# Scans that read PSUM, B products on GpSimd, and a new order of all steps, in an eight-layer network

## The reference

```python
A = -jnp.exp(A_log)
dA = jnp.exp(jnp.einsum('bld,dn->lbdn', delta, A))
dBu = jnp.einsum('bld,bln,bld->lbdn', delta, Bm, u)
def step(h, t):
    dA_t, dBu_t, c_t = t
    h = dA_t * h + dBu_t
    return (h, jnp.einsum('bdn,bn->bd', h, c_t))
_, ys = jax.lax.scan(step, h0, (dA, dBu, Cs))
y = jnp.moveaxis(ys, 0, 1) + u * Dp
```

## Time and profile before

| | |
|---|---|
| median of 3 runs | 1476.47 us (1473.23 to 1480.88) |
| the profiled execution | 1478.42 us, its span 1476.5 us |
| mean granted TensorE clock | 0.931 of full |
| busy share | PE 89%, DVE 72%, ACT 62%, POOL 42% |
| DMA | 82.88 MB moved |

### The profile page before, as it was taken

How to read it: one execution, slowest core, us unless ns; L and a number is a source line. 1 busy time by engine, 2 the same in 40 slices (tenths; PEclk the granted TensorE clock), 3 DMA queues, 4 the chain that set the end, 5 groups by cost and what they waited for, 6 DMA issues and landing times.

```text
span 1476.5 us, 25953 instructions
## 1 busy us (share of the span) xinstructions
PE 1307.9 (89%) x8638; PEld 924.5 (63%) x8638; DVE 1061.3 (72%) x3854; ACT 911.8 (62%) x2506; POOL 624.0 (42%) x637
## 2 busy tenths in 40 slices
PE   8324767987679999999999999999999999999998
PEld 4112445654446766776777776777778788875665
DVE  4998998588987478778347877559949769774334
ACT  5625687778664686756456778645758756664221
POOL 0002255532552365544545554744643433421744
PEclk9756789988879899999999999999999999999999
DMA  6777320105402001100100000020110000006230
GB/s 244 186 177 171 78 52 1 51 1 164 115 15 82 32 2 51 60 2 1 58 1 1 1 2 20 40 117 1 59 76 2 2 1 2 1 1 210 48 93 22
DMA packets 21788, 82.88 MB, mean 56 GB/s; under 512 B 1852, under 2 KB 8252, under 8 KB 19352
## 3 DMA queue, kind: packets, MB, share of 16 engines
q1 hardware_dynamic: 21656, 81.23, 18.8%
HBM read 77.88 MB, written 3.33 MB: 55 GB/s over the span
## 4 chain that ended last, share of the span: by engine, by line
PE 57%; DVE 26%; ACT 8%; issue 4%; POOL 3%; DMA 1%; SPq 0%; DVEq 0%; POOLq 0%; ACTq 0%
PE bank L888 49%; DVE arena L1559 7%; PE bank L892 7%; ACT arena L1321 5%; DVE arena L1726 5%; DVE arena L1797 2%; ACT L1321 2%; DVE arena L2056 2%; DVE arena L1795 2%; DVE arena L2049 1%; DVE arena L1565 1%; DVE stats L1573 1%; DMA arena<-cf 1%; DVE arena L1818 1%; DVE arena L1562 1%
## 5 line engine op out<-in xcount | busy, mean ns | idle before, releaser
L1321 ACT ACTIVATE arena<-arena 128x128 f32<-128x128 f32 (+2 forms) x792 | 347.7, 442 | 78.5 <-DVE arena L1797 54.9
L1321 ACT ACTIVATE arena<-bank 128x512 f32<-128x512 f32 (+4 forms) x378 | 202.7, 571 | 226.5 <-PE bank L888 139.4
L888 PE MATMUL bank<-XT,W 128*128 128x512 f32 (+1 forms) x752 | 292.6, 524 | 0.0
L2139 POOL TENSOR_TENSOR arena<-arena 128x256 f32<-128x256 f32 x192 | 121.0, 630 | 359.0 <-DVE arena L1812 357.9
L888 PEld LDWEIGHTS bank<-W,arena 128*128 128x128 f32 (+1 forms) x1888 | 233.5, 196 | 62.6 <-issue 40.1
L888 PE MATMUL bank<-arena 128*32 128x256 f32 (+8 forms) x2912 | 246.6, 347 | 21.4 <-ACT arena L1321 8.3
L888 PE MATMUL bank<-W,arena 128*128 128x128 f32 (+2 forms) x1888 | 246.1, 281 | 18.4 <-POOL arena L2112 6.0
L888 PEld LDWEIGHTS bank<-arena 128*32 128x32 f32 (+4 forms) x2912 | 162.3, 157 | 106.1 <-issue 73.0
L892 PE MATMUL bank<-CF,arena 128*128 128x128 f32 x1312 | 193.9, 289 | 37.0 <-POOL arena L2140 24.8
L2112 POOL TENSOR_TENSOR arena<-arena 128x512 f32<-128x512 f32 (+1 forms) x108 | 172.8, 1622 | 115.0 <-DVE arena L1559 56.1
L892 PEld LDWEIGHTS bank<-CF,arena 128*128 128x128 f32 x1312 | 158.3, 148 | 87.8 <-issue 58.2
(11 more groups left out here) (123 smaller groups left out, 1581.0 us busy)
## 6 DMA issues: line engine op xcount, KB each, us to landing
arena<-rep SPq DMA_DIRECT2D x62, 512.0 KB, 7.9
arena<-rws SPq DMA_DIRECT2D x8, 2048.0 KB, 7.3
arena<-rws SPq DMA_DIRECT2D x4, 1792.0 KB, 7.6
W<-w SPq DMA_DIRECT2D x2, 2124.0 KB, 8.3
arena<-rws SPq DMA_DIRECT2D x8, 384.0 KB, 10.7
W<-w SPq DMA_DIRECT2D x1, 2692.0 KB, 9.1
W<-w SPq DMA_DIRECT2D x1, 2256.5 KB, 9.3
rep<-arena SPq DMA_DIRECT2D x4, 512.0 KB, 4.8
```

Source lines behind the costliest of these rows:

```text
L888: return e.matmul(o, lhsT, rhs, start=start, stop=stop, skip_group_check=True)
L1321: return e.activation(o, a, func, **kw)
L2139: e.tensor_tensor(px[:, :, 0:128], px[:, :, 0:128], rec[:, :, 0:1].to_broadcast([128, 2, 128]), ALU.mult)
```

## The change

In "0.da" ScalarE writes the decays into a PSUM bank (role A, opened by the ScalarE step and held until "0.st" has scanned it) and not into the slot; a new need lets it run at most two states ahead of the scans. The scans read the bank. "0.bc" copies only B to SBUF; the bank with C stays open until the last "0.ac" of the chunk, and the product with C reads it there. The product with B is a GpSimd step of its own ("0.db") for the 62 states that come by DMA; the two that come by matmul keep it on VectorE. The scheduler counts banks for all engines now.

```diff
-                        own(tt(h, h, s0(c, 8), ALU.mult))
-                        on.wait_ge(*after("dA", "0.da", c, n))
-                        on.wait_ge(*own.last())
-                        for q in range(2):
-                            qs = slice(q * 256, (q + 1) * 256)
-                            own(e.tensor_tensor_scan(h[:, qs], dA[:, qs], h[:, qs], 0.0, ALU.mult, ALU.add))
-                    on.wait_ge(*emptied(u("c", "0.bc", c)))
-                    on.wait_ge(*own.last())
-                    tt(h, h, s0(c, 16), ALU.mult).then_inc(has["hc"], 1)
+                    else:
+                        on.wait_ge(*after("dB", "0.db", c, n))
+                    on.wait_ge(*after("dA", "0.da", c, n))
+                    ins = e.tensor_tensor_scan(h[:, 0:256], bank[a.i][:, 0:256], h[:, 0:256], 0.0, ALU.mult, ALU.add)
+                    if by_pe(c, n):
...
+                    else:
+                        own(ins)
+                    e.tensor_tensor_scan(h[:, 256:512], bank[a.i][:, 256:512], h[:, 256:512], 0.0, ALU.mult, ALU.add
+                                         ).then_inc(done[a.i], 1)
+                    on.wait_ge(*filled(cc))
...
+                    tt(h, h, bank[cc.i][:, :], ALU.mult).then_inc(has["hc"], 1)
```

```diff
-                        act(dA, dA, ACT.Exp, scale=am[:, g:g + 1], bias=am[:, 16 + g:17 + g]).then_inc(has["dA"], 1)
+                        steps_ = ring0(c, n)[:, 0:512]
+                    on.wait_ge(*free(a))
+                    act(bank[a.i][:, :], steps_, ACT.Exp, scale=am[:, g:g + 1], bias=am[:, 16 + g:17 + g]).then_inc(has["dA"], 1)
```

```diff
+                elif name == "0.db":
+                    h = ring0(c, n)[:, 512:1024]
+                    on.wait_ge(*repeated(c, n))
+                    on.wait_ge(*emptied(u("b", "0.bc", c)))
+                    e.tensor_tensor(h, h, s0(c, 8), ALU.mult).then_inc(has["dB"], 1)
```

The needs and the banks:

```diff
+HELD = {("0.bc", 0): [("c", 0, ("0.ac", 3, 0), 1, 1)], ("0.ac", 0): [("Y", 0, ("0.y", 0, 0), 4, 1)], ("1.pv", 0): [("Y", 0, ("1.y", 0, 0), 8, 1)],
...
+for _q in range(16):
+    HELD["0.da", _q] = [("A", 0, ("0.st", _q, 0), 0, 1)]
...
+            add("0.da", q, (by, q), ("0.a", 0, PREP), *([("0.st", q - 2)] if q >= 2 else []))
+            if by == "0.rp":
+                add("0.db", q, (by, q), ("0.bc", 0))
...
-                k = len(opened(x)) if g == "P" else 0
+                k = len(opened(x))
```

```diff
-         [(0, 2), (1, 2), (0, 3), (1, 3), (2, 2), (2, 3), (3, 2), (3, 3), (4, 2), (4, 3), (5, 2), (5, 3),
+         [(0, 2), (0, 3), (1, 2), (1, 3), (2, 2), (2, 3), (3, 2), (3, 3), (4, 2), (4, 3), (5, 2), (5, 3),
```

```diff
             load_x(2)
             e.dma_start(CF[:, 0:FIRST], cf[:, 0:FIRST]).then_inc(d_c, 16)
+            e.dma_start(W[0][:, 0:FIRST0], ws[0][:, 0:FIRST0]).then_inc(d_w[0], 16)
             load_x(0)
-            e.dma_start(W[0][:, 0:FIRST0], ws[0][:, 0:FIRST0]).then_inc(d_w[0], 16)
             load_x(1)
             e.dma_start(W[0][:, FIRST0:ws[0].shape[1]], ws[0][:, FIRST0:]).then_inc(d_late, 16)
+            e.dma_start(CF[:, FIRST:], cf[:, FIRST:]).then_inc(d_c2, 16)
             load_w(1)
-            e.dma_start(CF[:, FIRST:], cf[:, FIRST:]).then_inc(d_c2, 16)
```

More of the change, by code:

```diff
@@ L42 @@
 W_IN = {0: 0, 4: 0, 6: 0, 1: 1, 2: 1, 3: 1, 5: 1, 7: 1}
-CONSTS = [("ident", 128), ("one", 128), ("rows8", 128), ("mhalf", 20), ("cosk", 256), ("sink", 256), ("cosq", 256), ("sinq", 256), ("low", 128),
+CONSTS = [("ident", 128), ("mhalf", 20), ("one", 128), ("rows8", 128), ("cosk", 256), ("sink", 256), ("cosq", 256), ("sinq", 256), ("low", 128),
           ("stm", 384), ("relum", 384), ("outm", 384), ("offd", 384), ("early", 64), ("hm", 4)]
-FIRST = 404
+FIRST = 148
 FIRST0 = 1816
@@ L130 @@
 THIRDS = {1: 5, 4: 5, 6: 4}
-HELD = {("0.ac", 0): [("Y", 0, ("0.y", 0, 0), 4, 1)], ("1.pv", 0): [("Y", 0, ("1.y", 0, 0), 8, 1)],
+HELD = {("0.bc", 0): [("c", 0, ("0.ac", 3, 0), 1, 1)], ("0.ac", 0): [("Y", 0, ("0.y", 0, 0), 4, 1)], ("1.pv", 0): [("Y", 0, ("1.y", 0, 0), 8, 1)],
         ("4.pv", 0): [("Y", 0, ("4.y", 0, 0), 8, 1)], ("6.o", 0): [("out", 0, ("6.e", 0, 0), 8, 1)]}
 BLOCKS, SHARED, HIDDEN = {1: 8, 5: 8, 7: 14}, {1: 1, 5: 0, 7: 2}, {1: 4, 5: 4, 7: 5}
+for _q in range(16):
+    HELD["0.da", _q] = [("A", 0, ("0.st", _q, 0), 0, 1)]
 for _q in range(BEGIN[1]):
@@ L236, in stage_steps @@
                 add(by, q, ("0.wr", 0), *([("0.ac", (q - STATES) // 4)] if q >= STATES else []))
-            add("0.da", q, (by, q), ("0.a", 0, PREP))
-            add("0.st", q, ("0.da", q), (by, q), ("0.bc", 0), *([("0.st", q - 1)] if q else []))
+            add("0.da", q, (by, q), ("0.a", 0, PREP), *([("0.st", q - 2)] if q >= 2 else []))
+            if by == "0.rp":
+                add("0.db", q, (by, q), ("0.bc", 0))
+            add("0.st", q, ("0.da", q), ("0.db" if by == "0.rp" else by, q), ("0.bc", 0), *([("0.st", q - 1)] if q else []))
         for k in range(4):
@@ L333 @@
 TASKS = [[(s, 0) for s in range(8)], [(s, 1) for s in range(8)],
-         [(0, 2), (1, 2), (0, 3), (1, 3), (2, 2), (2, 3), (3, 2), (3, 3), (4, 2), (4, 3), (5, 2), (5, 3),
+         [(0, 2), (0, 3), (1, 2), (1, 3), (2, 2), (2, 3), (3, 2), (3, 3), (4, 2), (4, 3), (5, 2), (5, 3),
           (6, 2), (6, 3), (7, 2), (7, 3)]]
 AHEAD = {
[4 rows of a table removed]
-    (0, PREP): 67.31, (1, PREP): -869.94, (2, PREP): -782.64, (3, PREP): -77.67, (4, PREP): 246.56, (5, PREP): -616.95, (6, PREP): 195.78, (7, PREP): 842.21}
-URGENT = {
[9 rows of a table removed]
-LANDS = {("0.n", 2): 5.0, ("0.n", 0): 5.5, ("0.n", 1): 8.5, ("0.w", PREP): 8.0, ("0.a", PREP): 8.0, ("0.f", PREP): 8.0, ("0.b", PREP): 10.0}
[4 rows of a table added]
+    (0, PREP): -73.44, (1, PREP): 22.35, (2, PREP): -97.02, (3, PREP): 94.50, (5, PREP): -111.58, (6, PREP): 334.41, (7, PREP): 182.60}
+URGENT = {
[6 rows of a table added]
+    -36.44, "load": -56.09}
+LANDS = {("0.n", 2): 3.9, ("0.n", 0): 10.0, ("0.n", 1): 11.3, ("0.w", PREP): 8.6, ("0.a", PREP): 8.6, ("0.f", PREP): 8.6, ("0.b", PREP): 25.0}
 OVER = {4: (0,), 5: (1,), 6: (4,), 7: (3, 5)}
@@ L623, in group0, with by_pe @@
             return q % 4 * 4 + q // 4
+        def by_pe(c, q):
+            return c == BEGIN[0] and q < BEGIN[1]
         def repeated(c, q):
@@ L913, in _ @@
                     on.wait_ge(d_w[s], 16)
+                if name in ("0.ac", "0.b"):
+                    on.wait_ge(d_c2, 16)
                 if name in ("0.y", "0.h", "0.o", "0.b"):
@@ L969, in _ @@
                                  ring0(c, 4 * n + j)[:, 512:1024], n == 0, n == 3)
+                        if n == 3 and j == 0:
+                            ins.then_inc(done[uses["c", "0.bc", c, 0].i], 1)
                     ins.then_inc(full[b.i], 1)
@@ L1384, in _ @@
                 elif name == "0.bc":
-                    for b, k in ((u("b", name, c), 8), (u("c", name, c), 16)):
-                        evict(b, s0(c, k), bank[b.i][:, :])
+                    b = u("b", name, c)
+                    evict(b, s0(c, 8), bank[b.i][:, :])
                 elif name == "0.f":
@@ L1402, in _ @@
                 elif name == "0.da":
-                    dA, g = ring0(c, n)[:, 0:512], group0(n)
+                    g, a = group0(n), uses["A", name, c, n]
                     on.wait_ge(a_mat, 4)
-                    if c == BEGIN[0] and n < BEGIN[1]:
+                    if by_pe(c, n):
                         b = uses["b", "0.rb", c, n]
                         on.wait_ge(*filled(b))
-                        act(dA, bank[b.i][:, :], ACT.Exp, scale=am[:, g:g + 1], bias=am[:, 16 + g:17 + g]).then_inc(has["dA"], 1)
+                        steps_ = bank[b.i][:, :]
                     else:
                         on.wait_ge(*repeated(c, n))
-                        act(dA, dA, ACT.Exp, scale=am[:, g:g + 1], bias=am[:, 16 + g:17 + g]).then_inc(has["dA"], 1)
+                        steps_ = ring0(c, n)[:, 0:512]
+                    on.wait_ge(*free(a))
+                    act(bank[a.i][:, :], steps_, ACT.Exp, scale=am[:, g:g + 1], bias=am[:, 16 + g:17 + g]).then_inc(has["dA"], 1)
                 elif name == "0.h":
@@ L1706, in _ @@
                 elif name == "0.st":
-                    r = ring0(c, n)
-                    dA, h = r[:, 0:512], r[:, 512:1024]
-                    on.wait_ge(*emptied(u("b", "0.bc", c)))
-                    if c == BEGIN[0] and n < BEGIN[1]:
+                    h, a, cc = ring0(c, n)[:, 512:1024], uses["A", "0.da", c, n], uses["c", "0.bc", c, 0]
+                    if by_pe(c, n):
                         b, b2 = uses["b", "0.rb", c, n], uses["c", "0.rb", c, n]
                         on.wait_ge(*filled(b2))
+                        on.wait_ge(*emptied(u("b", "0.bc", c)))
@@ L1713, in _ @@
                         tt(h, bank[b2.i][:, :], s0(c, 8), ALU.mult).then_inc(done[b2.i], 1)
                         on.wait_ge(*emptied(b2))
-                        on.wait_ge(*after("dA", "0.da", c, n))
```

(15 more changed lines are left out.)

## The result

The changed kernel takes 1457.03 us (median of 4 runs, 1456.7 to 1458.54) against 1476.95: the ratio is 0.9867 (0.984 to 0.9893). A second series in the last group of experiments gave 0.9843 (0.9824 to 0.9861). So it is faster by 1.3 to 1.6%, some 20 us. The forecast was 1444, a gain of 32 us; the measured time lies 13 us above it, within the forecast's own 1428 to 1462.

The account below looks back on a forecast made before the run. VectorE's scans were taken to bound the first 500 us, PE's own work the rest. State gains and start, 41.5 us, less 3 (GpSimd) and 6 (banks) made 32; 1478.4 - 32 - 1.9 = 1444, range 1428 to 1462, 45%.

Parts of the forecast that it names:

- The regimes: Before 500 us VectorE is full and PE idle 146 us; behind, PE's own work, so early gains arrive almost whole.
- A PSUM input costs nothing: Scans and products reading a bank: bounds -1 to +10 us in all, taken as 0.
- Operations with both inputs in SBUF grow beside GpSimd: VectorE's scans grow from 0.637 to 0.824 us, SBUF products from 688 to 840 ns; forms with one PSUM input don't.
- the sum: State gains 9.9 before 110 us, 20 from 110 to 250, 10.6 for chunk 3, start 1: 41.5, less 3 and 6.
- what is late next is the DMA: 2.25 us: Where one chunk scans alone, a state's 512 KB take 2.25 us, so it gains 0.45 us, not 0.65.
- 0 on ScalarE: Writing decays to a bank: even at 1 us there are 2 states of room, 4.1 us; charged 0.
- The new order: 0: Steps behind layer 0: can give back at most the 22.8 idle us of PE there; put at 0.
- Banks: Scans beside layer 1's attention want 9 or 10 of 8 banks and take turns: 6 us charged, bounds 0 and 46.
- The clock comes back too: Rival: half of the 61 us that PE loses to its low clock in the first 500 us returns: 1414; 25%.
- The gain is absorbed: Rival: scans gain only the DMA's 0.45 a state, 29 us, and bank turns take 25: 1472; 11%.
- Slower: banks: Rival: layer 1's scores and the scans exclude each other at the full 46 us, a loss of 8: 1484; 14%.
- PSUM inputs are dear: Rival: bank inputs cost VectorE 50 ns more an operation, 1454, or 65 ns, 1456; 5%.

Follow-up runs that it names:

- new_operations_old_order: The changed kernel with lane order, AHEAD and URGENT of the kernel before, keeping its own operations, plan costs and first loads: 1463.14 us, ratio 0.9893.
- b_product_on_vector: The changed kernel with the product with B made by VectorE inside the scan step, none by GpSimd: 1475.79 us, ratio 0.9977.

## Why the prediction came out as it did

**The regimes were read right.** Among the runs with the changed kernel's order the last scan and the time move together: 220.9 to 239.3 us with the old operations, 18.4, and 21 us of time; 257.5, 36.6, and 36 us; 233.3 and 234.2, some 13, and 9 to 15 us. In another order they don't: new_operations_old_order ends its scans at 391.2 us and takes 1463. "Almost whole" was too much: of the 29 us gained before 500 us the order's idle time behind takes 9.

**A PSUM input costs nothing** was right: 684, 664 and 688 ns, where the undisturbed scans from SBUF in the earlier trace rows have a mean of 679 and the product 688. Without a B product on GpSimd (b_product_on_vector) the scans from a bank take 691 and 664. The rule of the Trainium skill on fixed costs (VectorE: DVE Perf Modes, "The TRN2 errata"), 65 ns more for a PSUM source, is not borne out by the scans either.

**Operations with both inputs in SBUF grow beside GpSimd** was right, and larger than the prediction used it: it counted the relief, and did not ask what the B products themselves would have done had the reads stayed in SBUF, 47 us of VectorE.

**The failing step is the size of the state's gain**, the three products 22 x 0.45, 24 x 0.93 and 16 x 1.32 of "the sum". With the shares that count and the 1 us of the start they came to 41.5 us, 32 after the charges. The operations measure 17.7 us of work brought ahead of 500 us in either order, and in time 16 us in the old order (1 to 0.9893) and 20 in the new one (1.0002 to 0.9867). Three things in these products did not come.

First, the refill. The term "what is late next is the DMA: 2.25 us" is the pace inside a refilled group, 2.1 to 2.2 us, and leaves out the break between groups. Alone, a state takes 2.61 us, since the ring of seven is refilled in fours and the chain from the sum to the next scan (1.97 + 4.89 + 1.27) is longer than the three states that are left in the ring, 3 x 1.97 = 5.9 us. So the lone chunk gains 0.09 us a state and not 0.45.

Second, the relief beside GpSimd. 0.28 of the 0.93 us and 0.67 of the 1.32 stood for collisions read in the old places. In the new order the old operations take 691 to 699 ns, so there was hardly any collision left to relieve. In the old order it was there, and the operations still brought no more than 17.8 us.

Third, new waits before the scans. The waits before GpSimd's products and before the first scans, from 50 to 250 us:


```profile
POOL arena L2118 <- DMA arena<-rep: 69.2, 38, 11.2
...
DVE arena L1728 <- ACT bank L1330: 13.7, 4, 5.0
...
DVE arena L1728 <- POOL arena L2118: 6.3, 7, 2.5
```

VectorE stands 20.0 us before first scans, 13.7 of them for ScalarE's decays. ScalarE is allowed two states ahead now, and its other work comes in between. Before the longest of these waits (4.96 us, ended at 105.69) it has two table loads, and three activations between them that wait for TensorE:

```profile
97.06 0.78 ACT L1330 ACTIVATE bank<-arena,am 128x512 f32<-128x512 f32 x1
97.86 1.28 ACT L1330 ACT_TABLE_LOAD   x1
...
103.51 1.28 ACT L1330 ACT_TABLE_LOAD   x1
104.81 1.48 ACT L1330 ACTIVATE bank<-arena,am 128x512 f32<-128x512 f32 x2
```

The prediction had put 0 on ScalarE, because 4.1 us of room is more than 1; the room is used up by other steps queued ahead. How the missing 14 us (32 less 17.7) divide among the three is argued, not shown: halving the bytes, or cutting the product to 8 columns, brought the last scan forward by 4.3 and 6.9 us only, and nothing tried more banks for the decays.

**"The new order: 0"** was nearly right for the wrong reason. It brings 11 us of TensorE's work ahead of 500 us and gives back 6 to 12 in idle time behind it. This is one of the prediction's own signs of being wrong: the part behind layer 0 has gained idle time, 22.3 to 31.5 us. The prediction looked at how much idle time the order could still remove there (22.8 us) and not at how much it could add.

**Banks** were charged 6 us with a bound of 46. No run shows a cost of the size of the bound; the old order with the new operations, where it had to appear, is within 0.5% of the changed kernel.

**The rivals.** "The clock comes back too" gave 30 us on top, and came in part. From 340 to 500 us the clock is 1.00, where it was 0.79 and 0.80 and TensorE had gaps beside chunk 3's scans; TensorE's busy total fell by 11.7 us, more than half of the 20. The sum had nothing for the clock and 32 us for idle time, which fell by 8.1. So the time came near the forecast in part by luck: a rival's term made up for some of what the sum's own terms lacked. "The gain is absorbed" gave 1472, as far off as the forecast, and its 25 us of bank turns appear in no run. "Slower: banks" and "PSUM inputs are dear" are refuted. GpSimd's products, read from the earlier trace rows as 1.04 to 1.22 us, take 1.26 to 1.27.

## What to carry to other kernels

Before an elementwise product is moved from VectorE to GpSimd, look at what VectorE runs beside it: with both inputs in SBUF both engines pay, and the move can lose as much as it should win; an input left in PSUM, where a matmul or ScalarE writes it anyway, kept these operations at their undisturbed time (684, 664 and 688 ns). Where a ring is refilled in groups, compare the refill's whole chain, not its bandwidth, with the time that the slots left will last. And a plan for all engines that is made anew has its own scatter (one such plan came out 32 us slower here), so an operation and an order are to be timed apart.

## What was not expected of the hardware

Operations with one tensor input can collide as well. Four VectorE operations on 128 columns of `X`, with scalars from `stats` in SBUF, which take 1.12 us at the undisturbed start of the same trace, took 4.72 us beside a row of GpSimd's products in the changed kernel, 131 to 136 us (start, us, engine, instruction):

```profile
6.55 1.12 DVE L1573 TENSOR_SCALAR arena<-X,stats 128x128 f32<-128x128 f32 x4 [1.20 <-POOL stats L2108]
...
129.92 6.15 POOL L2118 TENSOR_TENSOR arena<-arena 128x512 f32<-128x512 f32 x5
...
131.44 4.72 DVE L1573 TENSOR_SCALAR arena<-X,stats 128x128 f32<-128x128 f32 x4
```

The Trainium skill's page "SBUF — State Buffer", section "SBUF: two separate sides", counts VectorE's operations in a two-port mode, too, among those that want the shared pair. The slowdown agrees with it; no row says in which mode these four ran.

GpSimd's product of two different tensors of 512 columns takes 1.26 us undisturbed and not the 1.04 of the earlier trace rows, which is the square of one tensor. The normalising products (L2140 before), whose second input repeats one value along 256 columns, also begin at 1.03. So it is the same form in the profile at another price; the cause is not shown.
